# Layer 0's mixture of experts sorted over four batches instead of two, with raw rows reloaded for Pool and a new step order

## The chip, the cores and the metric

The kernel runs on one core of one Trainium2 chip. The metric is the device time of one execution in microseconds. The kernel before takes 1793.97 us, the median of three runs (1791.5 to 1795.19).

## What is computed

Two layers follow one another on 8 batches of 512 tokens of width 256. The change touches layer 0 alone: gated linear attention with 16 heads in chunks of 64, and beside it, on the same normalised rows, a mixture of 8 experts of which each token takes its best two.

```python
# layer 0, first half, for xn = layernorm(x), b = 8, t = 512, dim = 256
q, k, v = rmsnorm(xn @ Wq), rmsnorm(xn @ Wk), rmsnorm(xn @ Wv)
g, gt = xn @ Wg, log_sigmoid(xn @ Wgt) / 16
o = rmsnorm(chunk_gate_retention(q, k, v, gt, 64))   # chunks of 64, a state S per head
att = (silu(g) * o) @ Wo
# layer 0, second half
scores = softmax(xn @ gate_w); top = top_k(scores, 2)
scale[t, e] = scores[t, e] for the two chosen e, else 0
xs = scale.T[:, :, None] * xn                        # per expert
moe = sum_e (silu(xs @ w1[e]) * (xs @ w3[e])) @ w2[e]
x1 = x + att + moe                                   # and layernorm(x1) for layer 1
```

Layer 1 (a state space scan and a routed local and heavy attention) reads the normalised rows and x1 and is not changed.

## The kernel before

Each engine runs one in-order program, and all five programs are made from one list of steps. `L0_ORDER` (line 87) gives each kind of step a list of numbers, one for each batch and part. `ordered_plan` (line 345) sorts all steps of layer 0 by number, and each engine walks this list and emits the steps that are its own. The number is therefore not a time, only the place in each engine's queue. A step is named here by kind, batch or group, and part: `rld(0,1)` is the row load of batch 0, row tile 1. A row tile is 128 tokens, NT = 4 a batch.

The steps that matter here:

- SP issues DMAs: `x_ld` loads a batch's rows into XI (line 491; with batch 0 all weights, line 495; with batches 1 and 2 a `zero_fill`, line 534, of one of the two `sorted_scratch` halves, MT tiles of 128 KB, by the zeros of a constant tile), `rst` stores the gate rows (line 518), `rld` loads them back broadcast over the partitions into ROW (line 526, waits for the store and for the scan `dc` two row tiles back), `ld` and `yst` load a sorted tile and store an expert's output tile, `xx` loads x again into X, `x1s`, `xns` and `ss` store results.
- DVE: `bn`, `agg`, `xn1` normalise the input, `gl` and the gate steps follow, `qs` scales the queries, `dc` is the scan that makes the decays from ROW (2.3 us), `at` masks the scores, `n(g,0..10)` ranks the tokens of a group, `hd` multiplies in the experts.
- PE: `xt` transposes the input, `sm`, `qk`, `vg` project, `su` and `sr` sum and turn the gates, `kt`, `qt`, `qst` transpose, `sc`, `ou`, `cx`, `o` are the attention, `wo` the output projection. `tt`, `up`, `ht`, `dn` are an expert tile.
- ACT evicts and squares and does exp and silu. Exp steps and silu steps use two different activation tables. `EXP_STEPS` and `SILU_STEPS` name them, and a table is loaded whenever the list passes from one kind to the other.
- POOL: `sx` scales a row tile by one of its two expert weights (line 664), `sca` scatters it to its sorted places in DRAM (line 674), `gad` gathers the expert outputs and adds them to X (line 685), `rs1` and `rp` are the powers of -0.5.

The experts run in groups of GB = 2 batches: TT = 8 row tiles, each token twice, sorted by expert into tiles of 128 rows that hold one expert each. Rounding up costs up to E - 1 = 7 tiles, so a group has MT = 2 TT + 7 = 23 tiles, and four groups have 92. `sx` reads the normalised rows XN1, of which two batches are kept. All tiles of a group wait for all scatters of the group (`sorted_in`, line 475), and all gathers of a group wait for all its stores (`tiles_moved`, line 483). X has two slots a batch, XT two, XSC eight, XL six. The gathers add to X, then `ya` adds the attention, and then x1 is stored.

Layer 1 begins behind an all-engine barrier at the end of `layer0`.

Of the kernel before, what the change touches and what calls it, by code (L numbers as in the profile page):

```python
# [26 lines left out]
P = 128  # L27
# [53 lines left out]
def clear(nc, sems):  # L81
# [6 lines left out]
    "x_ld": [0, 22, 97, 270, 505, 988, 1329, 1719],  # L88
    "bn": [2, 3, 4, 1, 24, 23, 25, 26, 102, 104, 103, 101, 298, 272, 271, 300, 580, 579, 581, 570, 1107, 989, 990,
        1161, 1330, 1332, 1333, 1331, 1935, 1934, 1936, 1941],  # L90
    "agg": [5, 27, 113, 301, 619, 1173, 1352, 1942],
# [4 lines left out]
    "xta": [14, 52, 193, 631, 948, 1299, 1744, 2169],  # L96
    "xtv": [12, 45, 215, 629, 949, 1232, 1738, 2146],
    "sm": [15, 53, 236, 660, 971, 1354, 1770, 2181],
    "smc": [16, 65, 241, 664, 973, 1383, 1771, 2182],
# [10 lines left out]
    "src": [34, 176, 306, 816, 1028, 1598, 1807, 2316],  # L110
    "rst": [35, 190, 411, 864, 1380, 1629, 2223, 2478],
    "er": [39, 198, 304, 861, 1064, 1626, 1796, 2325],
# [189 lines left out]

I32 = mybir.dt.int32
GB = 2
TT = GB * NT
MT = 2 * TT + E - 1
GROUPED = {"pf", "n", "rg", "sx", "sca", "ld", "tt", "tc", "up", "si", "hd", "ht", "hc", "dn", "yc", "yst", "gad"}
# [45 lines left out]
def layer0(nc, x, w, scr, PB, const, load_ln_exp):  # L354
# [7 lines left out]
    with ExitStack() as ctx:  # L362
# [108 lines left out]
        def group_tile(b, t):  # L471

            return b // GB, b % GB * NT + t

# [2562 lines left out]
```

## Time and profile before

| | before |
|---|---|
| median of three runs | 1793.97 us |
| span of the profiled execution | 1782.7 us |
| mean granted TensorE clock over the span | 0.978 |
| PE, DVE, ACT, POOL busy over the span | 92%, 84%, 75%, 76% |
| layer 0, from the start to the barrier | 569.65 us |
| HBM read and written | 168.08 MB and 73.50 MB |

The profile is one execution. A matmul's busy time includes its way through the pipeline, so busy times of groups that follow closely add up to more than the engine's own busy time. The idle time before an instruction is put down to what released it. A group's line gives its busy time in us, the mean of one instruction in ns, and the idle time before it with what ended it.

### The profile page before, as it was taken

To read this page: it belongs to the slowest core of one execution; us is meant where nothing else is said; L and a number is where in the kernel's file an instruction comes from. 1 tells how busy PE (TensorE), PEld (TensorE's weight loads), DVE (VectorE), ACT (ScalarE), POOL (GpSimd) and SP (SyncE) were. 2 spreads that over 40 slices of the span, in tenths; PEclk is the share of its full clock that TensorE was granted. 3 is DMA by queue.
4 is the path that set the end of the run, shared out by engine and by line. 5 is a ranking of instruction groups with operands and counts; after the bars stand their busy time and mean duration, and the time that the engine had idled before them with its cause. 6 is when DMAs were issued, how large, how long until landed. Compare 5 with 4: busy or idle time off the path is not lost.

```text
span 1782.7 us, 44372 instructions
## 1 busy us (share of the span) xinstructions
PE 1631.9 (92%) x13580; PEld 1005.0 (56%) x13580; DVE 1494.5 (84%) x2798; ACT 1330.3 (75%) x3259; POOL 1353.8 (76%) x1114
## 2 busy tenths in 40 slices
PE   6999899899884888799999999999999999999988
PEld 4576585685673354355456456456556555544645
DVE  6848758668565999989989999999989999998997
ACT  4867666666652867968978987888897897797765
POOL 2807707618634078998999899899899999889996
PEclk9999999999996989999999999999999999999999
DMA  9446445645465843374373455446535446445430
GB/s 283 153 131 139 141 141 140 163 148 122 132 177 135 218 139 94 109 202 107 121 195 95 143 137 131 126 133 149 150 105 147 121 124 175 102 143 155 113 95 25
DMA packets 164993, 247.65 MB, mean 139 GB/s; under 512 B 30776, under 2 KB 109304, under 8 KB 164760
## 3 DMA queue, kind: packets, MB, share of 16 engines
q1 hardware_dynamic: 152472, 228.02, 45.9%
q0 software_dynamic: 12288, 16.79, 4.6%
q8 instruction: 114, 1.87, 0.5%
q14 instruction: 119, 0.97, 0.2%
HBM read 168.08 MB, written 73.50 MB: 136 GB/s over the span
## 4 chain that ended last, share of the span: by engine, by line
PE 31%; DVE 11%; issue 9%; ACT 8%; POOL 6%; DMA 2%; SPq 1%; DVEq 0%; POOLq 0%; ACTq 0%
PE bank L2323 28%; POOL HB L2274 3%; DVE bank L2846 3%; PE bank L2423 3%; DVE HB L2846 2%; POOL HB L2280 2%; DVE SU L2818 2%; ACT bank L2636 1%; ACT PR L2674 1%; DVE HB L2851 1%; ACT PT L2558 1%; DVE rows L2793 1%; DMA BC<-ssm_scratch 1%; ACT PR L2667 1%; PE bank L2451 1%
## 5 line engine op out<-in xcount | busy, mean ns | idle before, releaser
L2274 POOL TENSOR_TENSOR HB<-DD,BC 128x512 f32<-128x512 f32 x512 | 642.0, 1282 | 98.7 <-DMA DD<-SU 45.7
L2636 ACT ACTIVATE bank<-DD,A 128x512 f32<-128x512 f32 x512 | 349.6, 694 | 116.7 <-DVE HB L2851 74.2
L2280 POOL TENSOR_TENSOR HB<-HB,BC 128x512 f32<-128x512 f32 x256 | 324.9, 1285 | 31.2 <-DVE HB L2846 29.8
L2846 DVE TENSOR_TENSOR_SCAN bank<-bank,HB 128x512 f32<-128x512 f32 x256 | 310.7, 1214 | 23.5 <-ACT bank L2636 18.0
L2846 DVE TENSOR_TENSOR_SCAN HB<-bank,HB 128x512 f32<-128x512 f32 x256 | 309.8, 1210 | 7.8 <-ACT bank L2636 4.6
L2851 DVE TENSOR_TENSOR HB<-bank,BC 128x512 f32<-128x512 f32 x256 | 175.1, 684 | 15.9 <-DVE bank L2846 0.9
L692 POOL DMA_INDIRECT X<-expert_out_scratch,slot x64 | 111.1, 1736 | 66.2 <-DMA expert_out_scratch<-YS 39.4
L2323 PE MATMUL bank<-HB,fold 128*32 128x512 f32 x1024 | 137.0, 607 | 22.4 <-POOL HB L2280 10.9
L2423 PEld LDWEIGHTS bank<-ident,PR 128*128 128x128 f32 x768 | 86.7, 142 | 83.4 <-issue 44.9
L2423 PE MATMUL bank<-ident,PR 128*128 128x128 f32 x768 | 114.6, 281 | 18.8 <-ACT PR L2674 7.4
L2323 PE MATMUL bank<-XT,edge 128*128 128x512 f32 x256 | 122.7, 613 | 2.2 <-ACT XT L2558 2.0
L2323 PE MATMUL bank<-Wv,XRT 128*128 128x512 f32 x256 | 121.0, 608 | 0.8 <-ACT PT L2558 0.7
L2323 PE MATMUL bank<-Ka,Qa 64*128 64x128 f32 (+1 forms) x768 | 109.1, 404 | 13.5 <-ACT PT L2558 3.2
L2323 PE MATMUL bank<-XRT,Wk 128*128 128x512 f32 x256 | 120.0, 599 | 0.9 <-ACT PT L2558 0.8
L2558 ACT ACTIVATE PT<-bank 128x512 f32<-128x512 f32 x192 | 109.1, 598 | 10.8 <-PE bank L2423 8.0
L2323 PEld LDWEIGHTS bank<-PT,Va 128*64 128x64 f32 x1536 | 83.1, 137 | 38.8 <-issue 28.2
L2323 PE MATMUL bank<-PT,Va 128*64 128x128 f32 x1536 | 102.4, 279 | 2.0 <-ACT PT L2558 1.7
L717 PE MATMUL bank<-WX,XLT 128*128 x368 | 94.2, 393 | 7.5 <-issue 7.5
L2667 ACT ACTIVATE PR<-bank,nmax 128x128 f32<-128x128 f32 x256 | 90.9, 375 | 12.4 <-DVE nmax L2874 8.9
L2323 PE MATMUL bank<-Wao,OT 128*128 128x256 f32 x384 | 94.0, 388 | 0.8 <-DVE OT L2893 0.8
L682 POOL DMA_INDIRECT sorted_scratch<-XSC,slot x64 | 81.1, 1268 | 17.8 <-issue 14.9
L2674 ACT ACTIVATE PR<-bank,nmax 128x512 f32<-128x512 f32 x128 | 87.3, 688 | 5.8 <-DVE nmax L2877 3.7
(286 smaller groups left out, 3584.1 us busy)
## 6 DMA issues: line engine op xcount, KB each, us to landing
DD<-dd_scratch SPq DMA_DIRECT2D x488, 128.0 KB, 3.2
ROW<-row_scratch SPq DMA_DIRECT2D x64, 256.0 KB
BC<-ssm_scratch SPq DMA_DIRECT2D x128, 128.0 KB, 3.9
US<-us_scratch SPq DMA_DIRECT2D x32, 512.0 KB, 4.9
dd_scratch<-SU SPq DMA_DIRECT2D x16, 1024.0 KB, 5.5
us_scratch<-SU SPq DMA_DIRECT2D x15, 1024.0 KB, 6.5
XL<-sorted_scratch SPq DMA_DIRECT2D x92, 128.0 KB, 2.4
expert_out_scratch<-YS SPq DMA_DIRECT2D x92, 128.0 KB, 1.8
```

Source lines behind the costliest of these rows:

```text
L692: pool.indirect_dma_start(X[:, b % 2, t], None, scr["expert_out"][g % 2], bass.IndirectOffsetOnAxis(slot[:, g % 2, x, c:c + 1], 0), comput ...
L717: return pe.matmul(out, lhsT, rhs, start=start, stop=stop)
L2274: done(pool.tensor_tensor(HB[:, c % HR], du, bc, ALU.mult), "dbu")
L2280: done(pool.tensor_tensor(h, h, bc, ALU.mult), "cg")
L2323: return pe.matmul(out, lhsT, rhs, start=start, stop=stop)
L2423: q = pe.transpose(bank[:, j * P:(j + 1) * P], PR[:, m % 2, j * P:(j + 1) * P], ident[:])
L2558: done(act.activation(dst, banks.of[made, b, i][:], ACT.Copy), copy)
L2636: done(act.activation(PD[n % 2][:], delta, ACT.Exp, scale=A[:, k:k + 1]), "dA")
L2667: done(act.activation(PR[:, m % 2, cols], banks.of["score", b, m][:, cols], ACT.Exp, bias=nmax[:, m % 4, j:j + 1], accum_out=sums[:, m // ...
L2674: done(act.activation(PR[:, m % 2], banks.of["score", b, m][:], ACT.Exp, bias=nmax[:, m % 4, 0:1], accum_out=sums[:, a, h:h + 1]), "exp")
L2846: done(dve.tensor_tensor_scan(h if n % 2 else dA, dA, h, 0.0, ALU.mult, ALU.add), "scan")
L2851: done(dve.tensor_tensor(HB[:, (NCH * b + n) % HR], PD[n % 2][:], bc, ALU.mult), "mult")
```

## The change

GB becomes 4: two groups of TT = 16 row tiles, MT = 39 tiles each, 78 in all. The zero fills keep their places behind `x_ld(1)` and `x_ld(2)` and are 39 tiles long. As four batches' normalised rows are not kept, SP loads the raw rows of each row tile once more (new step `xr`, ring of three), and POOL's `sx` subtracts the mean and multiplies by weight times the reciprocal deviation in one instruction. The means and deviations of all batches are kept, and a twelfth rank step makes the products. X and XT have three slots, XSC and XL four instead of eight and six, QT, Q2, Q2T and KT two row tiles instead of four. For batches 0 and 1 the attention is added to x first and the gathers come later; for the others the order stays. PE loads the tiles' weight rows into registers in two halves of 20. All of `L0_ORDER` is replaced. In the diff the lists are cut to the kinds and places that the text speaks of.

```diff
 L0_ORDER = {
-    "x_ld": [0, 22, 97, 270, 505, 988, 1329, 1719],
-    "bn": [2, 3, 4, 1, 24, 23, 25, 26, 102, 104, 103, 101, 298, 272, 271, 300, 580, 579, 581, 570, 1107, 989, 990,
...
-    "rld": [51, 75, 168, 169, 220, 235, 320, 696, 731, 774, 853, 858, 866, 943, 944, 1473, 1498, 1503, 1652, 1653,
...
+    "x_ld": [0, 27, 62, 112, 277, 390, 470, 630],
+    "xr": [1, 2, 4, 535, 508, 576, 595, 633, 645, 681, 694, 738, 774, 767, 822, 832, 883, 886, 921, 1104, 1082, 1150,
...
+    "xx": [15, 13, 11, 14, 6, 5, 3, 7, 9, 8, 10, 12, 1894, 1865, 2052, 1913, 2127, 2140, 2122, 2131, 2101, 2162,
...
+    "bn": [17, 16, 18, 19, 36, 40, 38, 39, 86, 84, 88, 85, 207, 200, 197, 204, 312, 316, 314, 311, 441, 428, 443,
...
+    "gl": [42, 174, 267, 400, 629, 808, 922, 1730],
...
+    "sr": [51, 186, 332, 565, 648, 913, 1111, 1733],
...
+    "rst": [65, 198, 367, 579, 658, 918, 1133, 1751],
+    "qs": [67, 102, 77, 116, 223, 244, 292, 303, 433, 483, 613, 510, 667, 719, 789, 852, 947, 949, 1090, 1135, 1622,
...
+    "qst": [71, 107, 166, 214, 286, 297, 427, 478, 597, 503, 646, 709, 784, 810, 942, 945, 1085, 1131, 1619, 1461,
...
+    "rld": [80, 79, 118, 101, 228, 222, 264, 255, 374, 381, 442, 460, 604, 598, 749, 715, 892, 836, 1009, 1092, 1212,
...
+    "dc": [110, 92, 149, 165, 258, 248, 346, 366, 436, 457, 592, 557, 742, 706, 880, 824, 1002, 1075, 1197, 1285,
...
+    "n": [464, 468, 471, 474, 476, 477, 479, 481, 484, 486, 489, 490, 1017, 1025, 1029, 1034, 1036, 1038, 1040, 1041,
...
+    "sx": [529, 522, 493, 497, 568, 561, 586, 558, 627, 622, 638, 607, 673, 666, 680, 686, 730, 717, 766, 724, 765,
...
+    "ld": [933, 935, 937, 932, 952, 959, 956, 951, 1028, 1026, 1023, 1056, 1114, 1129, 1101, 1127, 1193, 1199, 1196,
...
-GB = 2
+GB = 4
 TT = GB * NT
 MT = 2 * TT + E - 1
+MTR = (MT + 1) // 2
...
-XNS, SXS, XLS, XSS, HSS, YSS = 2, 8, 6, 3, 3, 4
-RANKS = 11
+XNS, XTS, XS, XRS, SXS, XLS, XSS, HSS, YSS = 2, 3, 3, 3, 4, 4, 3, 3, 4
+RANKS, QS = 12, 2
+ATTENTION_FIRST = 2
...
+                def rows_load_raw(g, x):
+                    b, t = batch_tile(g, x)
+                    n = TT * g + x
+                    if n >= XRS:
+                        bb, xx = divmod(n - XRS, TT)
+                        after(sp, "sx", bb, 2 * xx, 2 * xx + 1)
+                    sp.dma_start(XR[:, n % XRS], x_rows(b, t)).then_inc(over[f"rows_in{n % XRS}"], 16)
...
                 def scaled_rows(g, i):
                     x, c = divmod(i, 2)
                     b, t = batch_tile(g, x)
                     after(pool, "n", g, RANKS - 1)
-                    after(pool, "xn1", b, t)
+                    k = TT * g + x
+                    pool.wait_ge(over[f"rows_in{k % XRS}"], 16 * (k // XRS + 1))
                     n = 2 * TT * g + i
                     if n >= SXS:
                         pool.wait_ge(moved[f"sort_in{n % SXS}"], 16 * (n // SXS))
-                    done(pool.tensor_scalar(XSC[:, n % SXS], XN1[:, b % XNS, t], weight[:, x, c:c + 1], None, ALU.mult), "sx")
+                    done(pool.tensor_scalar(XSC[:, n % SXS], XR[:, k % XRS], columns(mv1[:, :, 0], b)[:, t:t + 1],
+                                            scaled[:, x, c:c + 1], ALU.subtract, ALU.mult), "sx")
...
                 def add_expert_rows(g, i):
                     c, x = divmod(i, TT)
                     b, t = batch_tile(g, x)
-                    pool.wait_ge(over[f"xx_in{x}"], 16 * (g + 1))
+                    n = row_slot(b, t)
+                    if b < ATTENTION_FIRST:
+                        after(pool, "ya", b, t)
+                    else:
+                        rows_again_in(pool, b, t)
                     tiles_moved(pool, "y_st", YSS, g)
...
-                        after(act, "sc", b - 1, t)
+                        after(act, "sc", *lag(b, t, QS, NT))
```

## Rows read from the trace of the kernel before

**Rows 1.** Timeline at the seam: start us, us, engine, line, operation, idle before.
```profile
569.69 0.66 PE L2333 MATMUL bank<-ident,edge 128*128 128x128 f32 x2 [14.56 <-PEq L84]
```

**Rows 2.** Stretches: busy us of each engine (instructions), granted clock, DMA share, GB/s.
```profile
0.00:556.00 556.00, 494.40 (x7044) 360.19 (x7044) 373.11 (x1197) 345.55 (x1118) 291.81 (x264) 0.97 0.57 156
43.00:85.00 42.00, 41.12 (x793) 26.64 (x792) 36.99 (x109) 34.96 (x109) 37.33 (x34) 1.00 0.53 165
88.70:136.10 47.40, 43.55 (x359) 36.13 (x360) 18.58 (x58) 30.01 (x108) 1.01 (x1) 1.00 0.43 131
420.60:466.80 46.20, 41.40 (x772) 26.39 (x770) 34.35 (x92) 32.73 (x110) 39.89 (x35) 1.00 0.38 109
```

**Rows 3.** Groups of PE's instructions in layer 0, by shape.
```profile
L717 PE MATMUL bank<-WX,XLT 128*128 x368 | 94.2, 393 | 7.5 <-issue 7.5
...
L717 PE MATMUL bank<-WX,HT 128*128 x184 | 49.8, 385 | 0.3 <-ACT HT L1106 0.2
...
L885 PE MATMUL bank<-ident,XL 128*128 128x128 f32 x184 | 31.8, 288 | 6.0 <-DMA XL<-sorted_scratch 6.0
...
L899 PE MATMUL bank<-ident,HS 128*128 128x128 f32 x92 | 20.5, 274 | 1.1 <-DVE HS L1421 1.1
...
L717 PE MATMUL bank<-M,ones 128*128 128x8 f32 x8 | 1.5, 256 | 0.0
```

**Rows 4.** Timeline of SP's DMA issues at the start.
```profile
16.24 0.43 SPq L493 DMA_DIRECT2D edge<-in_L_attn_x  x1
16.71 0.55 SPq L536 DMA_DIRECT2D sorted_scratch<-zrow  x1
17.31 8.83 SPq L572 DMA_DIRECT2D X<-in_L_attn_x  x2
28.67 0.33 SPq L523 DMA_DIRECT2D row_scratch<-BR  x1
...
31.70 2.45 SPq L531 DMA_DIRECT2D ROW<-row_scratch  x4
...
34.83 0.51 SPq L536 DMA_DIRECT2D sorted_scratch<-zrow  x1
```

**Rows 5.** The same issues, 16 to 18 and 34.1 to 35.2 us: KB, us to landing.
```profile
sorted_scratch<-zrow SPq DMA_DIRECT2D x1, 2944.0 KB, 14.1
edge<-in_L_attn_x SPq DMA_DIRECT2D x1, 512.0 KB, 6.8
...
X<-in_L_attn_x SPq DMA_DIRECT2D x1, 128.0 KB, 13.9
...
sorted_scratch<-zrow SPq DMA_DIRECT2D x1, 2944.0 KB, 14.3
edge<-in_L_attn_x SPq DMA_DIRECT2D x1, 512.0 KB, 6.1
```

**Rows 6.** Timeline of DVE: the first scan of ROW.
```profile
36.81 2.29 DVE L1360 TENSOR_TENSOR_SCAN dec<-ROW,own_token 128x1024 f32<-128x1024 f32 x1
```

**Rows 7.** Timeline of PE at the start.
```profile
29.14 1.88 PE L717 MATMUL bank<-Wvg,XT 128*128 128x512 f32 x4
30.86 1.86 PE L717 MATMUL bank<-Wsm,XT 128*128 128x24 f32 x16
32.56 3.68 PE L717 MATMUL bank<-Wqk,XT 128*128 128x512 f32 x8
```

**Rows 8.** POOL's groups in layer 0, and the scale's spread.
```profile
L692 POOL DMA_INDIRECT X<-expert_out_scratch,slot x64 | 111.1, 1736 | 66.2 <-DMA expert_out_scratch<-YS 39.4 <-issue 15.9 <-DMA X<-expert_out_scratch,slot 10.9
L682 POOL DMA_INDIRECT sorted_scratch<-XSC,slot x64 | 81.1, 1268 | 17.8 <-issue 14.9 <-POOL XSC L672 2.5 <-DMA sorted_scratch<-XSC,slot 0.3
...
L672 POOL TENSOR_SCALAR XSC<-edge,weight x64: 913/964/3581, 43.1 to 462.1; 128x256 f32<-128x256 f32 x64
```

**Rows 9.** Timeline of ACT around a table load.
```profile
163.66 1.28 ACT L2976 ACT_TABLE_LOAD   x1
164.96 0.30 ACT L1076 ACTIVATE lr<-ssq,eps 128x12 f32<-128x12 f32 x1
```

More of the change, by code:

```diff
@@ L548, in tile_store @@
                     after(sp, "yc", g, j)
-                    for x in range(TT):
-                        if g >= 2:
-                            sp.wait_ge(moved[f"add{x}"], 32 * (g - 1))
+                    if g >= 2:
+                        group_added(sp, g - 2)
                     m = MT * g + j
@@ L615, in _ @@
                     sp.wait_ge(over[f"xn2_st{t}"], 16 * B)
-                for n in range(TT):
-                    sp.wait_ge(over[f"x1_st{n}"], 16 * B // GB)
+                for n in range(XS):
+                    sp.wait_ge(over[f"x1_st{n}"], 16 * NT * ((B - n + XS - 1) // XS))
                 sp.wait_ge(over["s_st"], 16 * B)
@@ L660, in input_rstd @@
                     after(pool, "agg", b, 0)
-                    after(pool, "xn1", b - 1, *range(NT))
-                    done(pool.tensor_tensor(rstd1[:], ve1[:], half[:, 0:NT], ALU.pow), "rs1")
+                    done(pool.tensor_tensor(columns(rstd1[:], b), ve1[:], half[:, 0:NT], ALU.pow), "rs1")
                 def scaled_rows(g, i):
@@ L778, in turn @@
                     after(pe, made, b, t)
+                    rows = src[:, t % QS] if what == "qst" else src[:, t]
                     bank = claimed(pe, what, b, t)
                     for k in range(ND):
-                        q = pe.transpose(bank[:, k * P:(k + 1) * P], src[:, t, k * P:(k + 1) * P], ident[:])
+                        q = pe.transpose(bank[:, k * P:(k + 1) * P], rows[:, k * P:(k + 1) * P], ident[:])
                     done(q, what)
@@ L1038, in scaled_queries_turned @@
                     after(act, "qst", b, t)
-                    after(act, "cx", b - 1, t)
-                    done(act.activation(Q2T[:, t].rearrange("p k i -> p (k i)"), banks.of["qst", b, t][:, 0:D], ACT.Copy),
+                    after(act, "cx", *lag(b, t, QS, NT))
+                    done(act.activation(Q2T[:, t % QS].rearrange("p k i -> p (k i)"), banks.of["qst", b, t][:, 0:D], ACT.Copy),
                          "qsc")
@@ L1312, in rank_step @@
                         if g >= 2:
-                            for x in range(TT):
-                                dve.wait_ge(moved[f"add{x}"], 32 * (g - 1))
+                            group_added(dve, g - 2)
                         own(dve.scalar_tensor_tensor(out=slot[:, g % 2, :, 0], in0=total[:], scalar=-1.0, in1=second[:],
@@ L1323, in rank_step @@
                     elif i == 9:
+                        q = dve.tensor_reduce(weight[:, :, 1], pick[:], X_AXIS, ALU.add)
+                    elif i == 10:
+                        q = dve.tensor_tensor(weight[:, :, 0], allw[:], weight[:, :, 1], ALU.subtract)
+                    else:
                         after(dve, "sx", g - 1, *range(2 * TT))
-                        q = dve.tensor_reduce(weight[:, :, 1], pick[:], X_AXIS, ALU.add)
-                    else:
-                        q = dve.tensor_tensor(weight[:, :, 0], allw[:], weight[:, :, 1], ALU.subtract)
+                        for c in range(GB):
+                            after(dve, "rs1", GB * g + c, 0)
+                        rates = rstd1[:, g * TT:(g + 1) * TT]
+                        q = dve.tensor_tensor(scaled[:], weight[:], bc(rates, 2), ALU.mult)
                     done(q, "n")
@@ L2991, in build @@
         moved = {n: ctx.enter_context(nc.semaphore(n)) for n in
-                 [f"sort_in{r}" for r in range(SXS)] + [f"add{x}" for x in range(TT)]}
+                 [f"sort_in{r}" for r in range(SXS)] + [f"add{x}" for x in range(XS * NT)]}
         edge = ctx.enter_context(nc.sbuf_tensor("edge", [P, 3 * NT * D], F32))
```

175 lines of the change are left out of this document (95 added, 80 removed), and 327 rows, old and new, of the table L0_ORDER.

## The prediction

> **What bounds the kernel now.** I read first where layer 0 ends, since the change touches nothing else. The timeline around the seam shows layer 1's first instructions on every engine at 569.65 us, behind a barrier that PE waited 14.56 us for [rows 1]. So layer 1 cannot overlap layer 0: what layer 0 gains or loses before that barrier is gained or lost by the whole kernel, and layer 1's 1213 us (1782.7 less 569.65) are carried over unchanged. Then the busy time by stretches [rows 2]: up to 556 us PE is busy 494.4 us (89%), DVE 373, ACT 346, POOL 292. PE is the engine that sets layer 0's length. Two kinds of stretch alternate. While Pool sorts (43 to 85 us, 420.6 to 466.8) PE is busy 41.1 of 42 and 41.4 of 46.2 us, with DVE at 37.0 and 34.4 and POOL at 37.3 and 39.9: four engines close together. While the sorted tiles run (88.7 to 136.1) PE is busy 43.6 of 47.4 us, with DVE under half and POOL nearly idle.
>
> **Part 1: 92 tiles become 78.** Each tile has on PE four matmul records from WX,XLT, two from WX,HT, two transposes of XL and one of HS. Their busy times [rows 3] are 94.2, 49.8, 31.8 and 20.5 us, together 196.3 over 92 tiles, 2.13 us each. This counts a little twice, because the groups' instructions overlap at their edges: the busy times of all 31 PE groups of layer 0 (the first and the last are in [rows 3]) add up to 576 us where PE was busy 494.4, a factor of 0.86. So a tile costs PE 1.83 us, and 14 tiles cost 25.6; without the correction 29.8, which is the upper end. The lower end is the rate at which these records can be issued at all: the smallest busy share, 0.86 of the two large groups alone, (94.2 + 49.8)/92 x 0.86 = 1.35 us, 19 us for 14. I take 25.6. ACT loses per tile four evictions (15 us in all for 14 tiles), DVE one product, SP a load and a store; none of these is the bound in a tile stretch, so they pay nothing more. The place and rank steps run twice on twice the columns instead of four times: under 2 us either way, taken as nothing.
>
> **Part 2: the first 65 us.** This is where I expect the gain to go. SP's queue at the start is bandwidth, not latency: the 128 KB load of X issued at 17.31 us, just behind the zero fill, landed 13.9 us later, with the zero fill itself (issued 16.71, 14.1 us) [rows 4, 5]. Its 2944 KB thus took 7.7 us; the second, behind an x_ld(2) that was issued as the ROW loads' issue ended at 34.15 and landed 6.1 later, at 40.3, ended at 49.1: 8.8 us. The new fills are 39 tiles long, 4992 KB: 13.1 to 14.9 us each, 10 to 12 us more for both.
>
> The new order puts much ahead of what is needed. (a) Between the weights and x_ld(1) now stand 15 loads of 128 KB (three xr, twelve xx), 1920 KB, 5.0 us at the fill's rate: x_ld(1) lands at about 28 instead of 23. DVE's bn(1) stands at steps 36 to 40 ahead of gl(0) at 42, which PE's sr(0) at 51 waits for; PE has then only three of the qk projections to do, and waits about 5 us. (b) zero fill 0 follows x_ld(1): lands at 28 + 13.1 = 41. x_ld(2) at step 62 can be issued at about 33 and lands at 42.6; zero fill 1 is issued with it and so stands **ahead of rst(0), step 65, and of the row loads rld(0,1) and rld(0,0), steps 79 and 80**. Before, the second fill stood behind them (rst and four ROW issues at 28.67 and 31.70, fill at 34.83 [rows 4]). It lands at 56 to 58. The store of the gate rows and the wait of rld for it (28.67 to 31.70 before, 3 us, of which 2 were fill) add 1 to 3, and one pair of ROW loads about 3: four ROW loads and x_ld(2), 1536 KB issued from 31.70, had landed at 40.3, 8.6 us, a third of it per pair. So dc(0,1), step 92, can start at about 61 us (58 to 65). Before, the first scan started at 36.81 [rows 6].
>
> What is queued behind it: on DVE, in its order, are dc(0,1) (2.29 us), xn1(2), qs(0,1) at 102 and all after. PE's qst(0,1) at step 107 needs qs(0,1), and all of PE is behind that. Ahead of 107 PE has xt(0), sm(0), four qk, four vg, sr, su, xt(1) and four transposing steps (qst, two qt, kt): by the start's timeline [rows 7] the second pair of qk ended at 36.2, after both xt, two sm, two vg, sr and su. The new order has one sm less (1.9), two vg more (2 x 1.9) and the transposing steps' twelve records, some 2 to 3 us at the 0.17 us a record of [rows 3]: 41, and with the wait of (a) 45 to 46. It goes on at 61 + 2.3 + 0.7 = 64, where 41 to 42 would have been the time of the same work before. The loss is **22 us** (16 to 26, by the bounds of the scan's start). ACT and POOL do not use it: POOL's first rows come only after n(0,11), step 490. DVE has as much to do afterwards as PE, so it does not catch up.
>
> **Part 3: Pool's sort.** Per row tile and choice it scales (964 ns) and scatters (1268) [rows 8]. The 16 pairs of the first group fill the stretch from 43.1 to 84.6 us, 41.5, those of the last 420.6 to 466.8, 46.2 [rows 2]: 2.6 to 2.9 us a pair. Now 32 pairs follow one another, 83 to 93 us, from step 490 to 932, where the first ld waits for all of them. Beside them PE has, counted along the plan, 8 qk, 8 vg, 14 o, 6 sc and the smaller steps, 76 us by each kind's busy time per step and the factor 0.86; its steps in the first sort stretch come to 39.2 us by the same count and took 41.5. So the cover is 81 us, and the sort ends 2 to 12 us after it. I take 3, since in the first group's stretch it is 2.6 us a pair that went with a PE busy throughout. The two operations (subtract, mult) in one instruction are not in the trace on POOL; the nearest row is the one operation, 964 ns. I take nothing for the second, the smaller of two guesses that the trace can't tell apart, with 0.96 us more (a second pass) as the upper end and nothing as the lower (a gain is excluded: the one-operation form is the shortest that the row shows). The ring XSC is four long, not eight: a scale waits until the scatter four places back has landed, and two scales and two scatters (4.6 us) stand between; the raw loads (32 of 128 KB, ring of three) are issued two row tiles ahead, over 10 us of Pool's work. A transfer that lands later than that adds to B below.
>
> **Part 4: the rest.** The new order alternates between EXP_STEPS and SILU_STEPS 47 times, not 29 (counted along the two plans), 18 more ACT_TABLE_LOADs of 1283 ns [rows 9], 23 us of ACT. As the 14 tiles take 15 to 18 us off ACT, its total stays at 346 + 6 of 540: hidden under PE, except where ACT is late. At the end, 32 gathers of 1.74 us [rows 8], 56 us, follow the last tile, beside 70 us of PE's attention by the count above; before it was 16. I take the 14.6 us after PE's last product [rows 1] as they are.
>
> **The sum.** 25.6 gained, 22 lost in Part 2, 3 in Part 3: 0.6 us less. That makes a span of 1782; the median lies 11.3 us above the span (1793.97 against 1782.7), which I carry over: 1793.4. With the fill's store round trip at its lower end the loss is 1 to 2 us smaller; forecast **1792 us**, for this case alone 1781 to 1804.
>
> **Rivals.** A, *the fill costs nothing*: if the 16 engines shared their time between transfers rather than take them in order, rst and rld would pass zero fill 1, only the 5 us of (a) would stay, and 25.6 less 5 and 3 would be kept, 17.6: 1776. For it: DMA is busy only half the time after 50 us. Against it: the 13.9 us of that X load. B, *the sort ends last* (the slower side): POOL's chain from n(0,11) to the last scatter replaces PE over steps 490 to 932. It decides from 2.6 us a pair (81 us over 32); at 3.3 us, a scale dearer by 0.6, the sort takes 106 us and the first tile comes 25 us late, 22 more than the forecast has, while SP, which waits in the same queue for xr, holds back rld: 1814. For it: 2.9 us a pair in the last group is over the mark. Against it: in the first group PE was busy 41.1 of 42 us beside it. C, *ACT is late*: if two in three of the 18 extra loads stand in a PE stretch that waits for ACT, 12 x 1.3 = 16 us: 1808. In the rows most loads are followed by the next activation at once, so that ACT pays the load and nothing around it.
>
> The Trainium skill (ScalarE: Activation LUTs, What ACT_TABLE_LOAD costs) puts every switch at 1283 ns for the load plus about 1380 ns of drain. By that rule C's 12 switches would be an estimated 32 us, not 16, and C would end at 1824. The trace speaks against the drain: the load at 163.66 ends at 164.94 and the next activation starts at 164.96 [rows 9].
>
> **How the numbers follow.** Chances: forecast case 0.42, A 0.18, B 0.27, C 0.13. The measurement can tell about 0.2%, 3.6 us. Within the forecast case (1781 to 1804) I give 0.18 to faster than 1790.4, 0.14 to within, 0.10 to slower than 1797.6. A is faster, 0.18. B and C are slower but for 0.04 within and 0.04 faster, where they are mild and meet the upper end of Part 1. Together faster 0.40, same 0.18, slower 0.42. For 8 in 10 the range runs from 1769 (A, with the 29.8 of Part 1 and the short scale) to 1816 (just over B).
>
> **What would show it.** Right: tiles' groups at x312 and x156 records with PE some 25 us less busy; the first dec scan at 58 to 65 us, PE idle for some 18 us before it, ROW loads issued only after 56 us. A is right if that scan starts before 45. B: PE waits for XL at the first tile for over 6 us, and pairs above 2.75 us. C: PE's and DVE's waits for ACT rise by over 10 us. Wrong altogether would be a layer 0 whose attention stretches are bound by DVE, which has then no tile stretches to recover in: its share of 37.0 in 42 us leaves only 5 us.

## The result, and the profile after

The changed kernel takes 1824.16 us (median of 4 runs, 1819.45 to 1825.28) where the kernel before took 1794.58 beside it: ratio 1.0164, 95% interval 1.0131 to 1.0197. It is slower by about 29 us, not even with it, and lies above the range. The profiled execution has a span of 1823.5 us with a mean clock of 0.961; the one of before had 1782.7 and 0.978. That is 41 us apart, 11 more than the medians are: the profiled run of before was one of its quick ones, so where the text below takes a size from the pair of profiles, it is a little large, and ratios of many runs decide. A number in us beside a ratio is the ratio times 1794.6. In one later batch (before_half_scale, one_op_drop) the kernel before itself took 1846 us, 52 more than here. It has no profile from that batch and the cause is not known; the ratios of that batch are not used.

Where the time went is told by the seam. Timeline of the changed kernel, to be laid beside [rows 1]:

```profile
610.55 1.73 PE L2380 MATMUL bank<-ident,edge 128*128 128x128 f32 x7 [9.95 <-PEq L84]
```

Layer 0 ends at 610.5 us, not at 569.6, and the rest takes 1213 us as before. All of it is lost in layer 0. Its stretches (columns as in [rows 2]; the two in the middle are the sorts of the two groups):

```profile
0.00:25.00 25.00, 10.42 (x31) 7.21 (x32) 9.36 (x24) 5.15 (x12) 9.66 (x38) 1.00 0.92 254
25.00:50.00 25.00, 16.57 (x70) 8.78 (x68) 10.14 (x47) 13.60 (x44) 2.02 (x2) 0.86 1.02 345
50.00:75.00 25.00, 6.24 (x85) 5.86 (x85) 7.97 (x17) 5.00 (x10) 0.00 (x0) 0.53 0.78 241
75.00:100.00 25.00, 24.10 (x564) 17.19 (x557) 24.05 (x83) 17.84 (x54) 1.01 (x1) 0.93 0.19 48
151.90:251.30 99.40, 82.21 (x1358) 55.41 (x1358) 69.69 (x222) 59.20 (x186) 86.04 (x66) 0.90 0.33 102
276.20:365.00 88.80, 78.57 (x914) 59.41 (x914) 32.71 (x86) 52.03 (x168) 77.58 (x64) 0.94 0.56 175
0.00:610.50 610.50, 491.16 (x6914) 345.98 (x6914) 365.28 (x1171) 355.31 (x1080) 305.48 (x269) 0.92 0.56 152
```

Three things stand out. Between 50 and 75 us no engine does a third of its time, and the granted clock falls to 0.53, near the lower of TensorE's two levels (1.2 of 2.4 GHz), and is still 0.93 in the next stretch. The sorts take 99.4 and 88.8 us, and POOL, not PE, is the busiest engine in the first. And over the whole of layer 0 PE is busy for 491.2 us, only 3.2 less than before [rows 2] although 14 tiles are gone, with the clock at 0.92 where it was 0.96 to the old seam.

The start, as the timeline of SP's issues shows it, to be laid beside [rows 4]:

```profile
25.54 0.43 SPq L518 DMA_DIRECT2D edge<-in_L_attn_x  x1
26.02 0.51 SPq L561 DMA_DIRECT2D sorted_scratch<-zrow  x1
36.51 3.45 SPq L518 DMA_DIRECT2D edge<-in_L_attn_x  x1
40.00 1.35 SPq L561 DMA_DIRECT2D sorted_scratch<-zrow  x1
41.40 14.58 SPq L548 DMA_DIRECT2D row_scratch<-BR  x1
60.73 2.46 SPq L556 DMA_DIRECT2D ROW<-row_scratch  x4
```

And the first scan on DVE, which was at 36.81 in [rows 6]:

```profile
65.78 2.29 DVE L1404 TENSOR_TENSOR_SCAN dec<-ROW,own_token 128x1024 f32<-128x1024 f32 x1 [16.99 <-DMA ROW<-row_scratch]
```

The second fill stands ahead of the row store, whose issue alone takes 14.58 us behind the two fills (0.33 in [rows 4]). The ROW loads wait for that store to land and go out only at 60.73, when the second fill has landed (60.5). The waits of PE in layer 0 (us in total, times, longest):

```profile
PE bank L821 <- DVE Q L1394: 21.1, 1, 21.1
...
PE bank L927 <- DMA XL<-sorted_scratch: 10.1, 4, 3.5
...
PE bank L941 <- DVE HS L1465: 9.2, 9, 3.0
PE bank L756 <- DVE AT L1414: 8.4, 1, 8.4
...
PE bank L805 <- DVE gt L1272: 6.1, 1, 6.1
```

And the longest waits of SP's queue, and POOL's scaling with the spread of its durations in ns (cf. [rows 8]: 913/964/3581):

```profile
SPq L570 <- POOL XSC L706: 119.6, 27, 10.3
```

```profile
L706 POOL TENSOR_SCALAR XSC<-XR,mv,scaled x64: 1208/1221/3562, 151.9 to 358.7; 128x256 f32<-128x256 f32 x64
```

The two-operation scaling takes 1221 ns at the median, 0.26 us more than the one of before. L570 is `xr`: SP stands 119.6 us for a free raw buffer, with ROW loads and `x_ld(7)` queued behind it (`x_ld(7)` goes out at 176.37, between two `xr` loads, and DVE waits 4.9 us for it; the expectation for ring6 below calls it x_ld(3), which was issued long before, at 69.7). So four suspects: the fills, the 15 loads ahead of x_ld(1), the ring of three, the second operation.

### The profile page after: what moved, and what is told of

Its sections match the earlier page's. It is cut to its first block, busy times and chain, and to the rows that moved or that the text cites. A ratio compares the mean times of both kernels' runs of the same rounds, so it can differ in the third digit from the quotient of the medians.

```text
span 1823.5 us, 43471 instructions
## 1 busy us (share of the span) xinstructions
PE 1631.7 (89%) x13450; PEld 992.6 (54%) x13450; DVE 1480.7 (81%) x2750; ACT 1339.8 (73%) x3221; POOL 1362.4 (75%) x1114
## 4 chain that ended last, share of the span: by engine, by line
PE 32%; DVE 11%; issue 8%; ACT 7%; POOL 5%; DMA 2%; SPq 1%; DVEq 0%; POOLq 0%; ACTq 0%
PE bank L2370 29%; DVE bank L2893 3%; POOL HB L2321 3%; PE bank L2470 2%; DVE HB L2893 2%; POOL HB L2327 2%; DVE SU L2865 2%; DVE HB L2898 1%; ACT bank L2683 1%; ACT PR L2721 1%; ACT PT L2605 1%; DMA dd_scratch<-SU 1%; ACT PR L2714 1%; DMA BC<-ssm_scratch 1%; PE bank L2498 1%
## 5 line engine op out<-in xcount | busy, mean ns | idle before, releaser
L2321 POOL TENSOR_TENSOR HB<-DD,BC 128x512 f32<-128x512 f32 x512 | 640.7, 1278 | 99.1 <-DMA DD<-SU 46.2
L2898 DVE TENSOR_TENSOR HB<-bank,BC 128x512 f32<-128x512 f32 x256 | 175.4, 685 | 15.9 <-DVE bank L2893 0.9
L706 POOL TENSOR_SCALAR XSC<-XR,mv,scaled 128x256 f32<-128x256 f32 x64 | 86.7, 1359 | 43.6 <-DVE scaled L1371 34.6
L695 POOL TENSOR_TENSOR rstd<-ve,half 128x4 f32<-128x4 f32 x8 | 8.2, 1024 | 124.9 <-DVE ve L1242 124.7
## 6 DMA issues: line engine op xcount, KB each, us to landing
sorted_scratch<-zrow SPq DMA_DIRECT2D x2, 4992.0 KB, 19.9
```

The lines of the kernel that those rows point to most:

```text
L706: done(pool.tensor_scalar(XSC[:, n % SXS], XR[:, k % XRS], columns(mv1[:, :, 0], b)[:, t:t + 1], scaled[:, x, c:c + 1], ALU.subtract, ALU. ...
L2321: done(pool.tensor_tensor(HB[:, c % HR], du, bc, ALU.mult), "dbu")
L2898: done(dve.tensor_tensor(HB[:, (NCH * b + n) % HR], PD[n % 2][:], bc, ALU.mult), "mult")
```

## The experiments

**Taking the suspects out of the changed kernel, one after the other.** fills_late:

```diff
-                        elif b < 3:
-                            zero_fill(b - 1)
+                        elif 4 <= b < 6:
+                            zero_fill(b - 4)
```

> The changed kernel with one edit: the two zero fills are issued behind x_ld(4) and x_ld(5), not behind x_ld(1) and x_ld(2). Theory S (the start): the changed kernel's PE stood still for 21.1 us at the first qst, and by the plan's step 201 it was 34 us later against its own work than the kernel before was. The ROW loads no longer stand behind a fill, so the first scan starts near 38 to 42 us instead of 67, PE's long wait goes, and with it the stretch at half clock behind it: 22 to 28 us back, 1796 to 1802 us. Rival E (the order sets the pace): the steps behind step 500 wait for Pool and SP whatever came before, so what the start gives back is waited away there: 10 us at most, 1814 or more. Nothing that the fills block at their new place (105 to 130 us) is expected, since ROW is two row tiles ahead there.

Measured: 1.0025 (1.0004 to 1.0046), 24.9 us better than the changed kernel. As theory S has it: the first scan starts at 42.61, PE's wait of 21.1 us is 1.3, and between 50 and 75 us PE is busy for 24.99 us at a clock of 0.90:

```profile
50.00:75.00 25.00, 24.99 (x581) 17.79 (x566) 23.83 (x84) 18.50 (x56) 1.01 (x1) 0.90 0.26 69
```

Nothing of it is seen to be waited away later, and E falls. start_mended moves the loads too:

```diff
-    "xr": [1, 2, 4, 535,
+    "xr": [27.1, 27.2, 27.3, 535,
-    "xx": [15, 13, 11, 14, 6, 5, 3, 7, 9, 8, 10, 12,
+    "xx": [122.1, 122.2, 122.3, 122.4, 122.5, 122.6, 122.7, 122.8, 122.9, 123.1, 123.2, 123.3,
```

> fills_late, and besides the three xr and the twelve xx loads are issued later: xr behind x_ld(1), xx behind step 122. By my step (a) the 15 loads put x_ld(1) 5 us back, and PE waited 6.1 us for the gates (sr): I expect 5 us less than fills_late, 1791 to 1797 if theory S holds. If PE's wait at sr has another cause, the same time as fills_late within 2 us.

Measured: 1.0006 (0.9983 to 1.003), 3.4 us better again; the direction fits, the difference alone is inside the intervals.

ring6:

```diff
-XNS, XTS, XS, XRS, SXS, XLS, XSS, HSS, YSS = 2, 3, 3, 3, 4, 4, 3, 3, 4
+XNS, XTS, XS, XRS, SXS, XLS, XSS, HSS, YSS = 2, 3, 3, 6, 4, 4, 3, 3, 4
```

> The changed kernel with XRS = 6 instead of 3, nothing else: the raw rows are loaded six row tiles ahead of Pool's scaling, so SP's xr steps find their buffer free. Theory Q (SP's queue): in the sort SP waited 119.6 us for Pool's scalings (27 waits, the longest 10.3 us) with the ROW loads and x_ld(3) queued behind them, and PE then waited 8.4 us for AT and 3.9 us for kvm, and DVE 4.9 us for x_ld. With six buffers these waits go: 12 to 18 us back with the cold clock behind them, 1806 to 1812. Rival B (Pool itself): the sort takes Pool 3.11 us a pair whatever SP does, and it is Pool's end that the tiles wait for: within 3 us of the changed kernel, 1821 to 1827.

Measured: 1.0135 (1.0094 to 1.0176), 5.2 us, between the two, and with some 9 us of uncertainty it does not tell them apart. SP's wait for POOL went as foreseen:

```profile
SPq L570 <- POOL XSC L706: 11.0, 8, 7.4
```

Of the 109 us that went, much came back in the same queue: SP's wait for the scans rose from 57.4 to 97.8 us, that for the gate rows from 33.1 to 55.7, and PE got little of it. The first sort took 94.9 us, not 99.4, the second 88.1; PE's wait for AT is still 7.0 us and its wait for the tiles is now 13.1 (9.9 at the start of the second group). POOL ends last there. all_mended is start_mended with this ring:

> start_mended and ring6 together. If the two losses are independent (theories S and Q) the gains add: about 1824 less 30 less 15, 1779 us, which would be faster than the kernel before by the 14 tiles' gain of my sum. If the pace is set by the order (E) or by Pool (B), the sum of the two is not reached: 1795 or more.

Measured: 0.9985 (0.9961 to 1.0009), 3.8 us better than start_mended, a difference inside the intervals. The gains measured one by one add up within the noise (32 us in all, 28.3 and 5.2 apart), but they are not the 45 expected, and 1779 is not reached: it equals the kernel before.

**The second operation.** mended_one_op, on top of all_mended:

```diff
-                    done(pool.tensor_scalar(XSC[:, n % SXS], XR[:, k % XRS], columns(mv1[:, :, 0], b)[:, t:t + 1],
-                                            scaled[:, x, c:c + 1], ALU.subtract, ALU.mult), "sx")
+                    done(pool.tensor_scalar(XSC[:, n % SXS], XR[:, k % XRS], scaled[:, x, c:c + 1], None,
+                                            ALU.mult), "sx")
```

> all_mended with a one-operation scaling on Pool (times the weight and rate only; the subtraction of the mean is left out of the results). In all_mended PE waited 9.5 us for the first tiles of the second group and 3.3 us for those of the first; the scaling took Pool 1221 ns where the one-operation form took 964. Theory B: 32 scalings fewer 0.26 us each are 8 us less a sort, the wait of 9.5 us shrinks to 1 or 2 and that of 3.3 goes: 8 to 12 us back, ratio 0.992 to 0.994. Rival: the sort waits for SP, DVE or the scatters' landings, or the time is lost next to the following wait: under 3 us, ratio 0.997 or more.

Measured: 0.9872 (0.9828 to 0.9915), 20.3 us better, twice the expectation. A second measurement in another batch:

> The kernel of mended_one_op once more (start mended, ring of six, one-operation scaling without the mean), so that its version with fewer tiles has a partner in the same batch. Every theory expects the 0.9872 again, within 0.003.

gave 0.9867 (0.9797 to 0.9938). The scaling falls from 1220 to 928 ns at the median, and what the sort takes falls with it, from 93.5 and 88.7 us to 84.2 and 77.1 (89.4 and 78.8 in the profile of mended_one_op_b, the same kernel). The stretches of the two sorts in mended_one_op:

```profile
122.30:206.50 84.20, 77.19 (x1261) 51.28 (x1261) 66.64 (x216) 55.38 (x173) 73.25 (x66) 0.90 0.37 121
231.90:309.00 77.10, 74.07 (x908) 56.97 (x908) 32.80 (x86) 51.09 (x166) 68.23 (x64) 0.98 0.64 201
```

The same edit on the changed kernel itself, one_op:

> The changed kernel as it is, with the one-operation scaling (the subtraction of the mean is left out of the results). From all_mended this edit took 20 us (0.9985 to 0.9872). If the second operation is a loss of its own, independent of the start and of the ring of raw rows, it takes 17 to 21 us here too: ratio 1.005 to 1.007 from 1.0164. If in the changed kernel SP's queue bounds the sort (its 119.6 us of waits), a shorter scaling is waited away: under 8 us, ratio 1.012 or more.

Measured: 1.0092 (1.0065 to 1.0119), 12.9 us: between the two expectations. Part of the shorter scaling may be waited away while SP's queue and the late start are still there; with some 8 us of uncertainty on the difference, this is not shown. The same work put into the kernel before, before_two_op:

```diff
-                    done(pool.tensor_scalar(XSC[:, n % SXS], XN1[:, b % XNS, t], weight[:, x, c:c + 1], None, ALU.mult), "sx")
+                    done(pool.tensor_scalar(XSC[:, n % SXS], XN1[:, b % XNS, t], eps0[:], weight[:, x, c:c + 1],
+                                            ALU.subtract, ALU.mult), "sx")
```

> The kernel before with one edit: Pool's scaling subtracts a column of zeros and multiplies by the weight (two operations, as in the changed kernel), 64 scalings, results unchanged. In the changed kernel such a scaling took 1.22 us where the one-operation form took 0.94 to 0.96. Theory B (Pool's sort paces the stretches in which it runs, in the kernel before too): 64 x 0.27 = 17 us more of Pool, most of it on the path: 10 to 17 us, ratio 1.0055 to 1.0095. The reading of my prediction (PE sets the length, the sort lies beside it and ends within a few us of it): under 4 us, ratio under 1.002.

Measured: 1.0108 (1.0079 to 1.0138), 19.4 us slower, at the upper end of theory B and a bit over. POOL's busy time in layer 0 rose by 20.8 us (295.8 to 316.6), somewhat more than the 17 worked out from the medians. Its sorts took 47.9 to 51.5 us instead of 41.5 to 46.2, and PE stood for the sorted rows, where in [rows 3] it was 6.0 us:

```profile
PE bank L886 <- DMA XL<-sorted_scratch: 24.0, 7, 8.1
```

So POOL's scaling was on the path of the kernel before already, beside a PE that was busy 41.1 of 42 us. Is it a bound in the other direction too? half_scale_b leaves the second scaling out. The one that stays takes the later of the two places in the list, and both scatters follow it:

```diff
-                    after(pool, "sx", g, i)
+                    after(pool, "sx", g, i - c)
...
-                                            XSC[:, i % SXS], None).then_inc(moved[f"sort_in{i % SXS}"], 16)
+                                            XSC[:, (i - c) % SXS], None).then_inc(moved[f"sort_in{i % SXS}"], 16)
```

> The kernel before with the second scaling of each row tile left out: its second scatter sends the rows scaled for the first choice, so the second choice's weight is left out of the results. 32 x 0.96 = 31 us leave Pool and nothing is put on another engine; before_act_scale, which moved them to ACT, came out 19 us slower because ACT once stood 11.7 us for a scatter's landing with PE 16.7 us behind it, and so did not tell. Theory B in both directions: the sorts of 41.5 to 46.2 us shrink by about 7 each, 10 to 20 us won, ratio 0.989 to 0.9945. Rival (the plan balances Pool against PE beside it): under 4 us, ratio 0.998 or more, while the same Pool work added cost 19 us.

It fell into the batch whose ratios are not used (0.9986 there). In its profile layer 0 ended at 637.1 us, and PE stood 39.0 us for instruction issue. Once more (566.0 and 19.9 us there):

> The kernel of before_half_scale once more (the kernel before without the second scaling of each row tile, the second choice's weight left out of the results), for the same reason. Theory B in both directions: ratio 0.989 to 0.9945. Balance (Pool costs when it grows and gives nothing when it shrinks): 0.998 or more; the first batch pointed here with 0.9986.

Measured: 0.9936 (0.9896 to 0.9976), 11.5 us won. The 32 scalings left out are 31 us at the row's 0.96, but POOL's busy time in layer 0 fell by only 23.3 us (295.8 to 272.5): the mean of those that stay rose from 1251 to 1688 ns, the median (980) hardly. The four sorts together are 21 us shorter (154 instead of 175). So adding POOL work costs nearly all of it and removing it gives about half: POOL and PE are both near the bound. How much of the missing half is due to the later places in the list is not told apart.

**Moving scalings to ACT.** act_scale takes 32 of the 64 from POOL (new step `sa`):

```diff
+                    done(act.activation(XSC[:, n % SXS], XR[:, k % XRS], ACT.Identity, bias=shift[:, x:x + 1],
+                                        scale=scaled[:, x, 1:2]), "sa")
```

> all_mended with the scalings for the second of the two choices, 32 of 64, moved from Pool to ACT (one activation with the rate as scale and minus mean times rate as bias; DVE makes the bias column in one more step of each group), results unchanged. all_mended gave 0.9985, and taking 0.28 us off each of its 64 scalings (18 us of Pool) gave 20 us. Theory B: 32 x 1.22 = 39 us leave Pool and the sort falls to 1.7 to 2.0 us a pair; PE and DVE then bound the stretch, so that somewhat more than the one-operation form is won: 20 to 30 us against all_mended, ratio 0.982 to 0.987. Rival (ACT in its order): ACT stands in its queue for the raw rows and for the ring of four XSC buffers, and what waits behind it on ACT (evictions of projections) comes late: 0 to 12 us, ratio 0.992 to 0.9985.

Measured: 0.9912 (0.9877 to 0.9947), 13 us better than all_mended and 16 us better than the kernel before, with the same results as both: the one version here that computes everything and is faster than either. Less than theory B had, more than its rival. Its sorts took 86.1 and 77.3 us, 2.7 and 2.4 a pair, not 1.7 to 2.0: POOL now waited 15.9 us for earlier scatters to land (2.1 in all_mended) and 10.7 for the rows that ACT scales. In the kernel before, the same move, as a Copy with the weight as scale, failed:

> The kernel before with the scalings for the second choice, 32 of 64, moved from Pool to ACT (a Copy with the weight as scale), results unchanged. In before_two_op 17 us more of Pool made the kernel 19 us slower, so every microsecond of its sorts lies on the path upwards. Theory B in both directions: 32 x 0.96 = 31 us leave Pool, the sorts (41.5 to 46.2 us) fall by about 7 us each until PE and DVE bound the stretch: 10 to 20 us won, ratio 0.989 to 0.9945. Rival (two engines side by side, the plan balanced between them): PE was busy 41.1 of 42 us beside the first sort, so Pool costs when it grows and gives nothing when it shrinks: under 4 us, ratio 0.998 or more.

Measured: 1.0105 (1.0072 to 1.0138). ACT's queue stood for the landing of a scatter, and PE stood 16.7 us behind it for QT:

```profile
ACT XSC L1009 <- DMA sorted_scratch<-XSC,slot: 14.4, 4, 11.7
```

That is a new wait, and says nothing on whether POOL bounds the kernel before, for which half_scale_b was made.

**The stall put into the kernel before.** before_fills:

```diff
-                        elif b < 3:
-                            zero_fill(b - 1)
+                        elif b == 1:
+                            for half in (0, 1):
+                                zero_fill("expert_out", half, 2 * TT)
+                                zero_fill("sorted", half, MT)
```

> The kernel before with the changed kernel's fills at their place: behind x_ld(1), ahead of the first row store, SP fills 2 x 39 tiles of DRAM with zeros (16 of each 39 into expert_out, 23 into sorted) instead of 23 and, behind the ROW loads, 23. Theory S: the ROW loads wait for 9984 KB where 2944 KB stood ahead of them; at 2.6 to 3.0 us per 1000 KB the first scan starts 18 to 21 us later, PE stands still for about 17 us, and the cold clock behind it adds some 3 to 5 us: 1812 to 1818 us, ratio 1.010 to 1.0135. Rival: the kernel before has slack behind its start (PE at 89%) that takes some of it back: under 1.007.

Measured: 1.0089 (1.0065 to 1.0112), 16 us: just under theory S, with an interval that reaches both. The first scan started at 57.20 (it waited 19.5 us for ROW), 20 us later than in [rows 6], and PE stood still for 18.5 us: here a little of the stall was taken back.

**The table switches.** mended_no_switch, for the gate's activation and the tiles' alike:

```diff
-                    done(act.activation(SG[:, t], VG[:, t, D:2 * D], ACT.Silu), "sg")
+                    done(act.activation(SG[:, t], VG[:, t, D:2 * D], ACT.Copy), "sg")
...
-                    elif what in SILU_STEPS:
-                        with_exp = False
```

> all_mended with both Silu activations of layer 0 (the gate's and the tiles') replaced by Copy of the same shape, which leaves the silu out of the results, and so without ACT's switches between the two tables in layer 0. all_mended gave 0.9985 of the kernel before, 23 us short of what Part 1 promised. Theory C (the switches): 47 switches of 1.28 us stand in ACT's queue, and each of them in a tile holds back HS or XLT; without them the tiles go back to 1.84 us (from 2.00) and 12 us or more are won: ratio 0.992 or less. Rival (the interleaving itself): ACT has 180 us to spare, the switches are hidden, and 0 to 5 us are won: 0.996 to 0.9985.

Measured: 0.9979 (0.9956 to 1.0002) against 0.9985, 1 us, inside the intervals. ACT had 48 loads in layer 0 of the changed kernel (61.6 us) and 30 before (38.5), 18 more as counted, and they cost nothing that can be measured.

**What a tile is worth.** before_drop, with MTD in place of MT in the counts of tiles as well:

```diff
+MTD = 20
...
-    return sorted(at, key=lambda step: at[step])
+    tile_steps = {"ld", "tt", "tc", "up", "si", "hd", "ht", "hc", "dn", "yc"}
+    return sorted((q for q in at if q[0] not in tile_steps or q[2] < MTD), key=lambda step: at[step])
```

> The kernel before with 12 of its 92 tiles left out (the last three of each group of 23: no load, transposes, products or evictions for them; SP stores 128 rows of zeros in their place, so their rows get nothing added). It measures what a tile is worth where the tiles run as in the kernel before. Part 1 of my sum put it at 1.83 us, bounds 1.35 to 2.13: 12 tiles are 22.0 us (16 to 26), a ratio to the kernel before of 0.988 (0.9855 to 0.991). Rival: tiles are partly hidden beside attention work that is bound by DVE or POOL, so that leaving them out gives under 14 us (ratio over 0.992), which would be a reason why the changed kernel's 14 tiles brought little.

Measured: 0.9942 (0.9921 to 0.9964), 10.4 us, 0.87 us a tile: the rival. In the profiles PE is busy 483.5 us up to the seam, 10.9 less than before, with the clock at 0.94, not 0.96:

```profile
0.00:565.00 565.00, 483.47 (x6937) 349.20 (x6938) 374.67 (x1207) 332.25 (x1071) 297.52 (x273) 0.94 0.56 153
```

The same with MTD = 33 of 39, mended_drop:

> all_mended with 12 of its 78 tiles left out (the last six of each group of 39, in the way of before_drop). In the kernel before 12 tiles fewer gave 0.9942, 10 us or 0.87 us a tile, not the 1.83 us that PE is busy for one. Theory B: in all_mended the path runs through the two sorts (93.5 and 88.7 us), and the first group's last tiles stand beside the second sort, so that their time is filled with waiting: only the six tiles of the second group count fully: 6 x 1.8 = 11 us and up to 3 more, a ratio to all_mended of 0.992 to 0.994, and so 0.990 to 0.9925 to the kernel before. If PE were the bound, 12 x 2.0 us = 24 us: 0.985.

Measured: 0.9966 (0.9948 to 0.9983), 3.4 us better than all_mended, 0.28 us a tile, less than either theory. Here PE's busy time did fall, from 482.2 to 462.0 us, and the time did not follow. Does POOL's sort hide it? one_op_drop, the same edit on mended_one_op, fell into the batch that is not used (0.9677; its own 1786.5 us were 17 above its second measurement, while the kernel before was 52 above):

> mended_one_op (0.9872) with the last six of each group's 39 tiles left out as in mended_drop. In all_mended 12 tiles fewer were worth 3.4 us, 0.28 us each. If Pool's sort covered them there (theory B), they are worth more once the sort is 20 us shorter: 8 to 20 us, ratio 0.976 to 0.983. If the worth of a tile beside attention work is small for another reason (ACT's and DVE's steps of a tile overlap, the clock falls when PE has less to do), it stays at 0 to 6 us: 0.984 to 0.9872.

Once more, with its partner beside it:

> The kernel of one_op_drop once more: in its first batch the kernel before itself took 1846 us, with PE's small products short of instructions, so that the ratio of 0.9677 says little. Against mended_one_op_b of the same batch: theory B 8 to 20 us for the 12 tiles, a ratio lower by 0.0045 to 0.011. The other theory (a tile's worth beside attention work is small whatever Pool does): 0 to 6 us, lower by at most 0.0035.

Measured: 0.9853 (0.9819 to 0.9886) against 0.9867, 2.5 us for 12 tiles, with an interval of some 14 us. That leans against theory B as the whole reason, but its 8 to 20 us are not excluded. What all three pairs show is a lower mean clock with fewer tiles, over all their runs: 0.9731 and 0.9707 for the kernel before and before_drop, 0.9706 and 0.9665 for all_mended and mended_drop, 0.9770 and 0.9698 for mended_one_op_b and one_op_drop_b. Layer 0 and layer 1 of mended_one_op_b, then of one_op_drop_b:

```profile
0.00:561.60 561.60, 480.16 (x6915) 338.08 (x6916) 365.41 (x1171) 354.62 (x1081) 288.63 (x273) 0.96 0.61 166
561.60:1773.00 1211.40, 1138.34 (x6536) 645.31 (x6536) 1114.03 (x1579) 983.79 (x2141) 1056.50 (x844) 0.99 0.48 132
```

```profile
0.00:547.70 547.70, 465.56 (x6807) 326.20 (x6808) 360.79 (x1159) 342.74 (x1033) 282.20 (x273) 0.93 0.61 167
547.70:1768.00 1220.30, 1147.22 (x6536) 648.48 (x6536) 1115.10 (x1579) 984.26 (x2141) 1056.71 (x844) 0.98 0.48 131
```

In this pair layer 0 is 14 us shorter without the 12 tiles, and layer 1, whose instructions are the same, 9 us longer at the lower clock. One pair of profiles doesn't make this an effect of the tiles: mended_one_op, the same kernel as mended_one_op_b, ended layer 0 at 551.5 us, only 4 later than one_op_drop_b, and layer 1 took 1220.5 us in half_scale_b too, which has all its tiles. Among runs of the kernel before, 0.001 of mean clock went with 0.9 to 1.8 us of time, by batch. By that rate 6 to 13 us of the missing gain would be the clock's; this is an estimate from a correlation, and no run here held the clock fixed.

## Why the prediction was wrong, point by point

The forecast was 1792 us and the range ended at 1816; measured were 1824. The sum had 0.6 us of gain and came out at 29.4 of loss. The step that failed is Part 3: the second operation of POOL's scaling, taken as nothing because PE was read as the engine that sets layer 0's length, was worth 20 of these 30 us (12.9 when taken out of the changed kernel alone). The sorts, taken to cost 3 us, were where the time went, and POOL beside PE was the bound. Of the rest, 6 us are Part 2, right in mechanism and short in size, and 4 are SP's queue.

The losses found, as a chain of ratios from the changed kernel to the last mended one; each difference carries some 5 to 9 us of uncertainty:

| step taken out | ratio after it | worth | forecast |
|---|---|---|---|
| changed kernel | 1.0164 | | |
| fills ahead of the ROW loads | 1.0025 | 24.9 us | 17 |
| 15 loads ahead of x_ld(1) | 1.0006 | 3.4 | 5 |
| ring of three (SP's queue) | 0.9985 | 3.8 | 0 |
| second operation | 0.9872 | 20.3 | 0 |
| what is left: 14 tiles fewer, and the rest of the order | | -23.0 | -25.6, and 3 for the sort |

The two rows in the middle (3.4 and 3.8) are not clear of noise, and the worths hold for this order of removal.

- **What bounds the kernel.** "PE is the engine that sets layer 0's length" is the step from which most went wrong. 89% busy was read as the bound. In before_two_op 17 to 21 us more of POOL cost 19, beside a PE that was busy nearly all along in the kernel before [rows 2]: the plan had filled each sort's stretch with as much PE work as fits, so a longer sort comes straight out at the first tile. The rows said it: four engines close together, and the tiles of every group wait for all scatters.
- **Part 3, mis-sized; rival B's mechanism.** I took nothing for the second operation, the lower of two guesses between 0 and 0.96 us. It is 0.26 at the median (0.29 between 1220 and 928 in the mended pair), inside the bounds, and it counts 64 times. I also followed only the first sort, 3 us over its cover; the second, 88.8 us long beside the first group's tiles, was not in the sum. The pairs took 3.11 and 2.77 us in the two sorts. Of the mark that I set for B, pairs above 2.75 were seen, and PE's wait at the first tile was 3.5 us, not over 6: the loss lay spread over the stretch, not in one wait. B's time of 1814, with the start as forecast, was the nearest of the four that were worked out from rows, in part by luck: it had a first tile 25 us late from a pair of 3.3 us, which was not seen.
- **SP behind xr.** Named under B, put at nothing in the forecast: 119.6 us of waiting in a queue, for which a ring of six gave 5.2 us in one place and 3.8 in the other, neither clear of noise.
- **Part 2, right in mechanism, 6 us short in size.** Every link was seen: x_ld(1) landed at 31.5 (28), the fills at 45.3 and 60.5 (41, 56 to 58), the scan started at 65.78 (61, bound 65) and PE went on at 68.8 (64). The first link was late because SP, at 0.43 to 0.78 us an issue, sent x_ld(1) only at 25.54. The second shortfall fits the clock behind the stall, which I had not priced. PE went on at 68.8, and the granted clock (the last but two) came back only here:

```profile
72.00:76.00 4.00, 4.00 (x75) 3.62 (x75) 2.75 (x13) 3.40 (x7) 0.00 (x0) 0.50 0.81 235
76.00:80.00 4.00, 4.00 (x51) 3.55 (x50) 3.50 (x8) 2.06 (x4) 0.00 (x0) 0.66 0.02 4
80.00:90.00 10.00, 9.99 (x287) 6.82 (x285) 9.79 (x39) 6.93 (x24) 0.00 (x0) 1.00 0.02 3
```

From these rows it is an estimated 5 us at most (half of the 7.2 us from 68.8 to 76, a third of the next 4); no run isolated it, and in before_fills a stall of 18.5 us cost less than itself. Measured 28.3 us against 22, which is about the uncertainty of the difference. Rival A (a fill costs nothing) is out.
- **Part 1, right only as a sum.** With all four losses out, the changed kernel is 23 us faster than the one before, near 25.6. But the step that led there, 1.83 us of PE a tile, isn't what a tile costs: 12 tiles alone gave 10.4 us in the kernel before and 3.4 in the mended one. The lower bound of 19 us for 14 was no bound, since it still took every microsecond of PE as time. At 0.28 to 0.87 us a tile, 14 tiles are 4 to 12 us, so 11 to 19 of the 23 us would come from elsewhere; two sorts in place of four, and with them two transitions fewer, are a likely place, but no run isolated them.
- **Part 4, right.** 18 more switches, hidden. Rival C is out: without any switch only 1 us was won. By the drain that the Trainium skill adds to each switch (ScalarE: Activation LUTs, What ACT_TABLE_LOAD costs) C was an estimated 1824 us, which is the measured time by chance. The tail of 14.56 us [rows 1] became 9.95.
- **DVE, open.** The prediction's last sign, attention stretches bound by DVE, was put to no run. In one such stretch of the changed kernel DVE is nearly as busy as PE:

```profile
100.00:150.00 50.00, 48.52 (x798) 31.49 (x800) 47.62 (x163) 33.86 (x107) 2.02 (x2) 1.00 0.34 93
```

What less DVE work would give in such a stretch is not known from these runs.
- **The offset of 11.3 us** between span and median was carried over; it was an accident of the run profiled, since here span and median agree within 1 us, and 11 us of the difference between the profiles is this.

## What to carry to other kernels

An engine at 98% beside another at 89% in a stretch that ends with both is no proof that only the first one counts: ask what the stretch's last consumer waits for, and price any work added to an engine that feeds it at its full duration, once it stands as close to the bound as POOL did here. A large transfer in a queue is paid by the first small one behind it whose result somebody needs, and it is cheap to move: the same fills some 60 us later (issued at 82.5 and 105.0) left no wait of PE that shows. Work that is removed beside other work is worth what a run with it left out says, not its busy time: 12 tiles, at 1.83 us of PE's busy time each, gave 10.4 us in one plan and 3.4 in another.

## What the runs showed of the hardware

- POOL's scaling of 128x256 in fp32 took 926 to 980 ns at the median with one operation and 1220 to 1234 with two (1234 in before_two_op, on normalised rows). Single ones took up to 4.6 us, so the means lie higher: 1251 and 1573 ns in the kernel before and before_two_op, 1040 and 1297 in mended_one_op and all_mended.
- While PE stood still for 21 us the granted clock fell, to 0.53 over the stretch from 50 to 75 us. With PE busy again from 68.8 it was still 0.50 from 72 to 76, 0.66 from 76 to 80, and 1.00 from 80 us on.
- With 12 tiles fewer the mean clock was lower in each of three pairs (0.9770 to 0.9698 in the widest). That this made the unchanged layer 1 longer is not shown: its 1220.3 us in one_op_drop_b are matched by 1220.5 in half_scale_b.
- On SP, the issue of the gate rows' store took 0.33 us in the kernel before and 14.58 us behind two fills. The two fills of 4992 KB took the queue for some 14 us each, from the landing ahead of them to their own (31.5 to 45.3, and 46.7 to 60.5).
